# Sixteen passes with a boundary after each, or one sequence of 256 head slots with the projections spread over it

## The reference, cut to what matters

```python
x = x + tanh(g_xattn[0]) * L0_xattn(layernorm(x), ctx, ctx, ...)   # attention with CoPE positions
x = x + tanh(g_ffn[0])   * L0_ffn(layernorm(x), ...)               # mixture of 8 experts and a shared one
x = x + tanh(g_xattn[1]) * L1_xattn(layernorm(x), ctx, ...)        # plain cross attention
x = x + tanh(g_ffn[1])   * L1_ffn(layernorm(x), ...)               # gated self attention
```

```python
gates = sigmoid(attn_logits)
pos = flip(cumsum(flip(gates, axis=-1), axis=-1), axis=-1)
pos = minimum(pos, npos_max - 1)
logits_int = einsum('bhqd,dn->bhqn', query, pos_emb)
logits_ceil = take_along_axis(logits_int, ceil(pos), axis=-1)
logits_floor = take_along_axis(logits_int, floor(pos), axis=-1)
w = pos - pos_floor
return logits_ceil * w + logits_floor * (1.0 - w)
```

## Time and profile before

| what | us |
| --- | --- |
| median of 3 runs | 5707.96 |
| range of the runs | 5701.75 to 5710.91 |
| the profiled execution | 5699.91 |
| its span | 5698.2 |
| granted TensorE clock, mean share of full speed | 0.721 |

### The profile page before, as it was taken

How to read it: one execution, slowest core, us unless ns; L and a number is a source line. 1 busy time by engine, 2 the same in 40 slices (tenths; PEclk the granted TensorE clock), 3 DMA queues, 4 the chain that set the end, 5 groups by cost and what they waited for, 6 DMA issues and landing times. The chain is left out here.

```text
span 5698.2 us, 64460 instructions
## 1 busy us (share of the span) xinstructions
PE 3375.8 (59%) x21126; PEld 2228.9 (39%) x21126; DVE 4138.4 (73%) x8874; ACT 2277.8 (40%) x5185; POOL 1398.0 (25%) x1125
## 2 busy tenths in 40 slices
PE   3256575655657566565665656556575665756576
PEld 2133352433435334352443534334352443524353
DVE  3878597685967858588585967859588585977853
ACT  2434344343434434344343443434344343443432
POOL 0322223131222312223131321312223131231310
PEclk7567686777768677686776867667786776868776
DMA  3000000000000000000000000000000000000000
GB/s 115 0 8 1 10 1 1 10 1 10 1 8 3 1 10 1 10 1 1 10 1 10 1 1 10 1 10 1 10 1 1 10 1 10 1 1 10 1 6 2
DMA packets 42741, 41.52 MB, mean 7 GB/s; under 512 B 6468, under 2 KB 42342, under 8 KB 42360
## 3 DMA queue, kind: packets, MB, share of 16 engines
q1 hardware_dynamic: 33144, 28.46, 1.7%
q10 hardware_dynamic: 9216, 8.39, 0.5%
HBM read 32.64 MB, written 4.19 MB: 6 GB/s over the span
## 5 line engine op out<-in xcount | busy, mean ns | idle before, releaser
L663 PE MATMUL banks<-xn,w 128*128 128x256 f16 x6912 | 958.4, 305 | 220.1 <-ACT h L734 220.1
L585 DVE COPY_PREDICATED banks<-masks,banks 128x448 f32<-128x448 int16 (+5 forms) x1536 | 1031.2, 671 | 74.9 <-PE banks L381 14.0
L514 POOL TENSOR_TENSOR steps<-slope,rises 128x512 f32<-128x512 f32 x256 | 295.3, 1154 | 2686.3 <-DVE masks L577 2384.5
L663 PEld LDWEIGHTS banks<-xn,w 128*128 128x128 f16 x6912 | 740.8, 109 | 419.3 <-ACT h L734 245.5
L470 ACT ACTIVATE core_prob<-z,negmax 128x256 f32<-128x256 f32 x512 | 255.9, 503 | 570.0 <-DVE negmax L609 569.4
L554 DVE TENSOR_TENSOR_SCAN c<-gate,cap 128x514 f32<-128x514 f32 x256 | 323.6, 1264 | 183.3 <-ACT gate L446 183.3
L521 POOL TENSOR_TENSOR neg_rest<-shift,c 128x512 f32<-128x512 bf16 x256 | 298.3, 1165 | 464.0 <-DVE masks L577 423.3
L676 PE MATMUL banks<-w,a 128*128 128x256 f32 x1152 | 313.6, 421 | 104.2 <-DVE o L838 66.4
L525 POOL TENSOR_TENSOR partial<-partial,core_scores 128x512 f32<-128x512 f32 x256 | 365.9, 1429 | 1.2
L603 DVE TENSOR_TENSOR_SCAN z<-keep,steps 128x512 f32<-128x512 bf16 x256 | 328.8, 1284 | 40.7 <-issue 38.7
L577 DVE TENSOR_SCALAR masks<-shift 128x512 int16<-128x512 int16 x1536 | 335.4, 290 | 7.8
(11 more groups left out here) (254 smaller groups left out, 6846.6 us busy)
## 6 DMA issues: line engine op xcount, KB each, us to landing
stage<-in_L_ffn_w SPq DMA_DIRECT2D x16, 512.0 KB, 5.1
z<-in_ctx ACTq DMA_DIRECT2D x32, 128.0 KB, 2.7
core_pT<-in_x ACTq DMA_DIRECT2D x32, 128.0 KB, 3.0
u<-in_ctx SPq DMA_DIRECT2D x32, 128.0 KB
x<-in_x SPq DMA_DIRECT2D x32, 128.0 KB
out<-x SPq DMA_DIRECT2D x32, 128.0 KB, 1.7
stage<-in_L_ffn_w SPq DMA_DIRECT2D x8, 256.0 KB, 7.1
stage<-in_L_ffn_sw SPq DMA_DIRECT2D x2, 512.0 KB, 4.4
```

The source lines that it names most:

```text
L514: nc.gpsimd.tensor_tensor(k.steps[:], k.slope[:], k.rises[:, h % 2], ALU.mult).then_inc(sem["core_steps"], 1)
L585: move = nc.vector.copy_predicated(tab[:, :, 0:S - b], k.masks[:, n, :, 0:S - b], tab[:, :, b:S])
L663: last = nc.tensor.matmul(k.bank[bank][:, f * S:(f + 1) * S], w[:, e, a, c, par, f * P:(f + 1) * P], k.x_parts[:, b, c, :], start=(n == 0) ...
```

## The change

The passes are gone. Sixteen batches are one sequence of 16 x 16 = 256 head slots, written out in full and followed by 19 more, without barriers and without clearing. Every wait gets the value that its semaphore has reached before the batch (`raised_by(b)`), so each engine keeps a running count. The side of batch b starts in slot 16b+19 and has exactly 16 slots. Its pieces start at 0 (none is run ahead of the slots): 3, 3, 3, 3, 3, 3, 3, 4, 2, 22, 13, 3, 3, 20, 14, 4. I number these slots 0 to 15.

```diff
-PIECE_TIMES = [4] * (4 + 2 * NE) + [2] * 2 + 2 * ([6] * 4 + [0.5] * (H + 1) + [1.2] * (H + 1) + [5] * 3)
-EARLY = 2
-SLOTS = H + 3
-PIECES = [0] * SLOTS
-PIECE_TIMES = PIECE_TIMES[EARLY:]
+PIECE_TIMES = [5.6] * (4 + 2 * NE) + [2] * 2 + 2 * ([6] * 4 + [0.5] * (H + 1) + [1.2] * (H + 1) + [5] * 3)
...
+LAG = 3
+PIECES = [0] * H
...
+AHEAD = [1, 0, 0, 1, 2] + [1] * (H - 5)
+G = B * H
+SLOTS = G + H + LAG
+
+
+def side_pieces(s):
+
+    return (PIECES[(s - LAG) % H], FIRST[(s - LAG) % H]) if s >= H + LAG else (0, 0)
+
+
+def ahead_pieces(s):
+
+    return AHEAD[s % H] if s >= 4 and s < G + 4 else 0
...
-        run_pass(nc, k, 0, None)
-        with nc.Fori(1, B) as i:
-            run_pass(nc, k, i, i - 1)
-        run_pass(nc, k, None, B - 1)
+        zero(nc, k)
+        all_batches(nc, k)
```

The core's loads and projections become a third generator, `ahead`, of 15 pieces a batch. Batch 0's run before the first slot; the others run one at the end of most slots, behind the core and the side, in the batch before. They use one bank (2) where there were four, so each product waits for the copy of the one before:

```diff
+def ahead_tensor(nc, k, pe, b):
...
+    for m in range(P // HB):
+        if m >= 1:
+            pe.wait_ge(sem["core_q_stack"], at["core_q_stack"] + m)
+        stack_pair(nc, k, 1, k.core_k_parts, m, bank).then_inc(sem["core_k_stack_psum"], 1)
+        yield
+        pe.wait_ge(sem["core_k_stack"], at["core_k_stack"] + m + 1)
+        stack_pair(nc, k, 0, k.core_q_parts, m, bank).then_inc(sem["core_q_stack_psum"], 1)
+        yield
```

More of the change, by code:

```diff
@@ L493, in core_scalar @@
+        for _ in range(pieces - first):
+            next(side)
+        if s < G:
             act.wait_ge(sem["core_moved"], s + 1)
@@ L1182, in _ @@
+            store(B - 1)
         @block.gpsimd
         def _(pool):
-            side = side_pool(nc, k, pool) if rest is not None else iter(())
-            if core is not None:
-                core_pool(nc, k, pool, side)
-            for _ in side:
-                pass
+            side = chain.from_iterable(side_pool(nc, k, pool, b) for b in range(B))
+            ahead = chain.from_iterable(ahead_pool(nc, k, pool, b) for b in range(B))
+            for _ in range(sum(AHEAD)):
+                next(ahead)
@@ L1190, in _ @@
+            core_pool(nc, k, pool, side, ahead)
         @block.tensor
         def _(pe):
-            side = side_tensor(nc, k, pe) if rest is not None else iter(())
-            if core is not None:
-                core_tensor(nc, k, pe, side)
-            for _ in side:
-                pass
+            side = chain.from_iterable(side_tensor(nc, k, pe, b) for b in range(B))
+            ahead = chain.from_iterable(ahead_tensor(nc, k, pe, b) for b in range(B))
+            for _ in range(sum(AHEAD)):
+                next(ahead)
@@ L1207, in _ @@
[L1207 to L1208 removed]
+            side = chain.from_iterable(side_scalar(nc, k, act, b) for b in range(B))
+            ahead = chain.from_iterable(ahead_scalar(nc, k, act, b) for b in range(B))
+            for _ in range(sum(AHEAD)):
+                next(ahead)
+            core_scalar(nc, k, act, side, ahead)
         @block.vector
         def _(dve):
[L1212 to L1215 removed]
@@ L1216, in _ @@
-            for _ in side:
-                pass
-            if core is not None:
-                core_tail(nc, k, dve, step)
+            side_step = stepper(dve, sem["dve_side"])
+            core_step = stepper(dve, sem["dve_core"])
+            side = chain.from_iterable(side_vector(nc, k, dve, side_step, b) for b in range(B))
+            ahead = chain.from_iterable(ahead_vector(nc, k, dve, core_step, b) for b in range(B))
+            for _ in range(sum(AHEAD)):
+                next(ahead)
@@ L1220, in run_pass @@
+            core_vector(nc, k, dve, core_step, side, ahead)
     zero(nc, k)
```

731 lines of the change are left out of this document (409 added, 322 removed).

## The result

The changed kernel takes 5498.5 us (median of 4 runs, 5495.3 to 5510.2) where the kernel before takes 5706.5 beside it: a ratio of 0.9639, 95% interval 0.9623 to 0.9656. It is faster, by 3.6%, and not by the 8.8% forecast; 5498 lies above the range, in the band of the rival in which the side holds the core.

The account below looks back on a forecast made before the run. DVE was taken to bound the kernel, its work having holes at each pass's turn. 370 us at the start, 15 batches of 309, less 18, plus 211.5 gave 5198.5, stated as 5208 us (8.8% less); range 4850 to 5430.

Parts of the forecast that it names:

- the side holds the core: Rival: core work behind side pieces loses another 5 us in slots 9, 10, 13, 14; 329 us a batch, 5508; chance 0.13.
- What bounds the kernel: Middle pass before the change: one engine's work, DVE's 255 us, with 88 us of holes, 53 of them at the turn.
- The constants: Outside the full batches: first scan at 171, first side at 370, then 18 off for draining and 211.5 for the end.
- Slots 0 to 8, 167: Pieces 0 to 26, mostly experts: 153.4 us before, 167 with output heads, tail wait and `ahead`; DVE over 90% busy.
- slot 12, 27: Gated setup in one slot for two: 35.7 - 9.8 = 26 us, plus 1 for waits with less cover.
- Slots 9 to 11, 40 + 17: Cross attention: pieces 27 to 61 in two slots for three, 40 us for 49.7; its end in slot 11 stays 17.
- Slots 13 to 15, 58: Pieces 68 to 105, gated attention to the store: 47.6 us plus 19.6 of core, less 9 for filled waits, 58.
- The stall goes to the table product: Gate scan's waits go; moves wait for the table product in slots 10 and 14 instead, some 5 us each.
- The order of ACT gives nothing in slots 0 to 8: New order of PE and ACT saves nothing in these slots, since DVE is at 91% there.
- Store and load of x at nothing: Between batches: the addition to x comes some 7 us behind its last write, so cost nothing; uncovered, 1 to 3 us.
- DVE beside POOL: L829 and L832 slow beside POOL, at most 12 us a batch; three expert parts there before and after, so no gain.
- The better cover: Rival: PE and ACT run ahead over slot ends, 279 us a batch, 4758; band 4758 to 5060; chance 0.32.

Follow-up runs that it names:

- `ahead` moved: Changed kernel with the pieces of `ahead` taken from slots 9, 10, 11 and 13 and put behind lighter slots: 5414.3 us, ratio 0.9518.
- weights of 4.8: Changed kernel with weight 4.8 for 5.6 on a batch's first 22 side pieces: 5279.0 us; with `ahead`'s pieces also off the heavy slots, 5207.7 us.
- the early slope: Kernel with `ahead`'s pieces moved, plus slope copy and table product directly behind the fifth side piece in slots 10 and 14: 5443.5 us.

## Why the prediction was wrong, point by point

**What bounds the kernel.** Right: DVE's work with holes in it. The variants that compute the same have DVE busy for 248 to 254 us a batch and differ in the holes.

**The constants.** Right to 5 us: the first gate scan at 168 (171), the second batch's projections and 19 slots to 374.7 (370), and from the last full batch's end to the span's end 507 us (309 - 18 + 211.5 = 502.5). The single bank, bounded from 0 to 27 and taken at 17 without a row, cost 18: from the preamble's last write of DVE to the first gate scan are 43.6 us where they were 25.6. That the scan comes 3 us earlier than forecast is due to the preamble, which ends 3.9 us sooner, and which I had left as it was.

**Slots 0 to 8, 167.** 170.1, and slot 12, 27: 29.0. Right within 3 and 2 us. DVE is busy for 87% of slots 0 to 8, less than the 90% that I had named as a sign.

**Slots 9 to 11, 40 + 17.** 66.7, and this is the first failed step: `ahead`'s pieces cost nothing on PE and ACT in my sum. The check on it, the chain of 24.6 us less "one crossing less, some 5 us", leaves 20; the chain took 27.4, and still 23.1 in the mean with `ahead` moved, so that it was some 3 us short by itself. I had put `ahead`'s pieces, 6.2 us of DVE, into slots 0 to 8 and cost them on that engine alone; on the engines of the chain there is one at the end of each of the slots 9, 10 and 11. Moved away, the sum is 57.3. Among the rivals I had a neighbour of the mechanism, PE waiting for ACT's copy with the next slot's transposes behind it. PE hardly waits there, 5.1 us in all over the 512 products for the stacks:

```profile
L319 PE MATMUL banks<-ahead,select 32*128 32x256 f16 x512 | 125.7, 394 | 5.1 <-ACT core_keys L326 2.8 <-ACT core_queries L326 2.1 <-ACT core_offset L499 0.3
```

It is ACT that waits for PE, 1.7 us a piece, and this is paid where PE and ACT are the chain. The first wait, taken at 1.85 us because it was that in a slot that had begun with other pieces, was 5.40: it depends on which piece a slot begins with, and was to be read from the list of pieces. The maxima came 19.9 us into slot 9 even so, for the 18.5 taken; the rest of the miss is behind them.

**Slots 13 to 15, 58.** 67.0, the second failed step: "I take off 9", for core work that fills DVE's wait of 14.36 us. None of the 9 came. In parts, before and after: to the split maxima 15.0 and 22.0, the chain 22.2 and 29.9, from there to the store, or the slot's end, 10.5 and 15.1. The sum grew by 19.4, as much as two core slots take by themselves. Of the 7.0 us ahead of the maxima 4.85 are the wait for the first scores, which a stack a slot earlier takes away (slot 13 is 24.1 us in the change and 19.8 with it, slot 12 2.7 longer). DVE's core work did run in the wait, but ACT's core work of two slots lies in the chain, and DVE's next moves wait for what follows it. I had said that ACT and PE are the chain and taken 9 off nevertheless, with no row for it. The overlap can be had in another order of the pieces: at weights of 4.8 with `ahead` moved, where the chain holds the core work of one slot, the stacks are in slot 12 and piece 65 is in slot 11, slots 13 to 15 take 56.2 us and 12 to 15 79.7, less than my 58 and 85.

**The stall goes to the table product.** Right in kind: the gates' waits went, the moves' waits came. Wrong in place and size: in front of slots 11 and 15 and not in 10 and 14, and 9.7 to 13.5 us for the 5 I gave. What it means is shown by the early slope: it is not a cost, only a place.

**The order of ACT gives nothing in slots 0 to 8.** Right, and with the gates behind again the whole is the same within the interval.

**Store and load of x at nothing.** Right: no wait of DVE's L1005 for a DMA in the trace; in slot 0 it waits 4.1 to 4.4 us for the product of the tail, taken at 3.0.

**DVE beside POOL.** L829 took 983 ns in the mean before and as L943 983 after, L832 989 and as L946 981. The sum was right to get nothing from it. Whether the rule of the Trainium skill (SBUF — State Buffer, Who interferes with whom) is what sets 1.64 against 0.68 us was not tried; it moved nothing here.

**The clock** was in no term. I read rows with 0.50, 0.64 and 0.81 beside them and took durations from all of them alike. In the run with doubled scores 4.5 us of slot 11 lie between batches at 0.55 and at 0.82 with the same instructions.

**The rivals.** "The side holds the core" gave 329 us a batch and 5508 for slots 9, 10, 13 and 14, by 5 us each; it had 0.13. That it comes within 10 us of the time is luck: its size was a guess from half a wait, the loss was met in slots 11 and 15, and half of its cause, the place of slope and table product, is refuted by the early slope. The better cover, at 0.32, has nothing for it: no stage was faster than in my sum but slots 9 and 10 taken alone (35.2 us for 40), whose chain ended in slot 11.

**What stays open.** Why the clock is up in slot 11 of one batch and not of the next with the same instructions, and what would bring it up in slot 10 for less than it costs: work added ahead of it did not, a third product inside it did in some batches. How much of the gain at 4.8 is the clock's (slot 15 takes 23.2 us at 0.94 and 29.2 at 0.68 in the same kernel) and how much the shorter chain's. And what piece 102 in slot 14 is worth by itself.

## What to carry to other kernels

When work is spread over the slots of an in-order schedule, cost each piece on the engine that bounds that slot, not on the one that bounds the kernel; a handshake at a slot's end that costs nothing in most light slots is paid in full, and here the clock fell with it, where PE and ACT are the chain. Count how many slots' core work stands inside each chain: a last piece that slips over a slot's end takes one more in. An idle time in front of an instruction tells where a chain is met, not what it costs: undo the wait and look at the next one before counting it. Which piece stands first and last in each slot belongs beside the slot's bound in the working: moving two pieces by one slot each was worth 76 us.

## What the runs showed of the hardware

- Fewer matmuls can take longer: 64 fewer of 1306 in a batch, and PE was busy for 213.9 us instead of 205.9, at a granted clock of 0.68 instead of 0.73.
- The granted clock of one slot differs from batch to batch in one run, 0.55 to 0.82 in slot 11, and its length follows, 31.4 to 26.9 us, with the same instructions.
- Products added ahead of a slot did not raise the clock in it: with doubled scores and 12 further products PE was busy for 15.1 to 16.7 us of slot 9 instead of 11.2 at most, and slot 10 was at 0.50 as without. A third product for every two inside the slot raised it to 0.68 to 0.71 in five batches of 14.
